# Another set of whole tiles, other slots for some jobs, and one ScalarE raise for two heads

## The reference, cut to what matters

```python
ffn  = lambda z: z @ W.T + b + (z @ V_r) @ C.T                # rank 32
x = x + 0.5 * ffn(ln(x))                                      # stage A
q, k, v = split(ln(x) @ W_attn)                               # stage B, 16 heads of 16
s = (q @ k.T) / 4, causal
p = (s*s + 1 if s > 0 else 1 - s/100) / 1000                  # 'polymax', no row sum; for s >= -100
x = x + (p @ v) @ W_proj                                      # stage C
x = x + 0.5 * ffn(ln(x))
```

## Time and profile before

| what | us |
| --- | --- |
| median of 3 runs | 1784.87 (1782.54 to 1789.83) |
| the profiled execution | 1781.97 |
| its span, first to last instruction | 1780.2 |
| TensorE's granted clock, mean over the span | 0.983 |

### The profile page before, as it was taken

How to read it: one execution, slowest core, us unless ns; L and a number is a source line. 1 busy time by engine, 2 the same in 40 slices (tenths; PEclk the granted TensorE clock), 3 DMA queues, 4 the chain that set the end, 5 groups by cost and what they waited for, 6 DMA issues and landing times.

```text
span 1780.2 us, 67010 instructions
## 1 busy us (share of the span) xinstructions
PE 1610.6 (90%) x27158; PEld 834.3 (47%) x27158; DVE 1328.6 (75%) x3272; ACT 1364.4 (77%) x2178; POOL 1319.1 (74%) x1415
## 2 busy tenths in 40 slices
PE   5788889998999999999999999999999989998884
PEld 3444444454545454554545455554545443434342
DVE  4776787778787878787787878778787778786661
ACT  2355668898888888888787887888897879797660
POOL 3456568888988878788897878788796768685652
PEclk9999999999999999999999999999999999999997
DMA  3453343324334252443334152433425141413102
GB/s 95 159 169 120 109 144 89 116 73 123 92 115 127 60 166 72 133 112 110 111 107 138 55 170 77 124 94 110 130 80 147 46 118 41 118 41 94 40 29 64
DMA packets 156857, 183.17 MB, mean 103 GB/s; under 512 B 22140, under 2 KB 129788, under 8 KB 155012
## 3 DMA queue, kind: packets, MB, share of 16 engines
q1 hardware_dynamic: 156548, 178.82, 34.4%
HBM read 101.38 MB, written 76.30 MB: 100 GB/s over the span
## 4 chain that ended last, share of the span: by engine, by line
PE 55%; DVE 16%; ACT 12%; issue 6%; POOL 6%; DMA 3%; SPq 1%; ACTq 0%; POOLq 0%; DVEq 0%
PE y_ps L1079 20%; PE bank L1079 16%; PE score L1079 16%; DVE rp L1012 9%; ACT rp L910 5%; ACT rp L926 3%; POOL rp L807 3%; PE bank L1105 3%; DVE lin L1018 2%; DMA x1c<-x_scratch 2%; POOL z L769 1%; DVE bnst_ln L1037 1%; ACT rp L930 1%; ACT lin L916 1%; POOL rp L782 1%
## 5 line engine op out<-in xcount | busy, mean ns | idle before, releaser
L1012 DVE TENSOR_SCALAR rp<-score 128x512 f32<-128x512 f32 (+2 forms) x1728 | 944.3, 574 | 287.0 <-PE score L1079 284.2
L807 POOL TENSOR_TENSOR rp<-rp 128x1024 f32<-128x1024 f32 (+1 forms) x416 | 757.3, 1829 | 57.9 <-DVE rp L1012 46.1
L1079 PE MATMUL score<-qs,ks 96*32 96x512 bf16 (+3 forms) x10240 | 725.1, 350 | 54.2 <-DVE lin L1018 22.7
L1079 PE MATMUL y_ps<-rp,vt 128*16 128x512 f32 (+3 forms) x5120 | 598.7, 533 | 27.2 <-POOL rp L807 11.3
L910 ACT ACTIVATE rp<-score 128x512 f32<-128x512 f32 (+1 forms) x832 | 463.5, 602 | 201.5 <-PE score L1079 199.5
L1079 PEld LDWEIGHTS score<-qs,ks 96*32 96x32 bf16 x10240 | 303.4, 96 | 432.7 <-DVE rp L1012 146.0
L926 ACT ACTIVATE rp<-rp,rise 128x1024 f32<-128x1024 f32 (+1 forms) x416 | 466.4, 1155 | 0.4 <-POOL rp L782 0.4
L782 POOL TENSOR_SCALAR_AFFINE_SELECT rp<-rp 128x256 f32<-128x256 f32 (+1 forms) x384 | 186.4, 487 | 291.3 <-DVE rp L1012 163.4
L930 ACT ACTIVATE rp<-rp 128x1024 f32<-128x1024 f32 (+2 forms) x224 | 291.8, 1308 | 83.9 <-POOL rp L782 57.2
L1018 DVE SCALAR_TENSOR_TENSOR lin<-score,slope_mask 128x128 f32<-128x128 f32 x768 | 215.3, 280 | 0.0
L1079 PEld LDWEIGHTS y_ps<-rp,vt 128*16 128x16 f32 x5120 | 143.2, 96 | 116.4 <-issue 38.3
(11 more groups left out here) (79 smaller groups left out, 1292.1 us busy)
## 6 DMA issues: line engine op xcount, KB each, us to landing
qs<-part_scratch SPq DMA_DIRECT2D x384, 64.0 KB, 2.4
ks<-part_scratch SPq DMA_DIRECT2D x384, 64.0 KB, 2.4
part_scratch<-parts SPq DMA_DIRECT2D x12, 1536.0 KB, 5.6
state_scratch<-st_new SPq DMA_DIRECT2D x16, 528.0 KB
st<-state_scratch SPq DMA_DIRECT2D x64, 132.0 KB
x_sb<-in_L_attn_x_dram SPq DMA_DIRECT2D x16, 512.0 KB, 4.5
x_scratch<-x SPq DMA_DIRECT2D x16, 512.0 KB, 5.6
qT_scratch<-qkT SPq DMA_DIRECT2D x16, 512.0 KB, 5.6
```

What stands on the lines that cost most here:

```text
L807: pool.tensor_tensor(half, half, half, ALU.mult).then_inc(squared["pool"], 1)
L1012: nc.vector.tensor_scalar(rp[T % RP_BUFS][:, 2 * u + v, off:CH], score[H % S_BUFS][:, v, off:CH], 0.0, RISE, ALU.max, ALU.add).then_inc(ra ...
L1079: return nc.tensor.matmul(*args, start=start, stop=stop, skip_group_check=True)
```

## The change

The list of whole tiles becomes 13 tiles instead of 14, seven off the diagonal (6, 10, 26, 28, 33, 34, 38) and six on it (3, 17, 20, 23, 31, 35). Before, the list was 10, 16, 22, 28, 33, 38 and 2, 3, 9, 11, 20, 23, 35, 39. Seven table entries move by one to three slots. `JOINT` holds the odd halves of the 17 tiles that are off the diagonal and shared; for these `heads_at_once` gives one pair, and so one raise of 1024 columns that waits for the second head's score, and its counters rise by two. `HALVED` is empty; with that, `pool_squares` is the same as `shared`, and the branches for it never run.

```diff
-WHOLE = OFF_DIAG[3::4] + [t for t in DIAG if TILES[t][2] >= 2 * P]
+WHOLE = [3, 6, 10, 17, 20, 23, 26, 28, 31, 33, 34, 35, 38]
+
+HALVED = []
+
+JOINT = [2 * t + 1 for t in OFF_DIAG if t not in WHOLE]
 
 def shared(T):
-    return T % NT not in WHOLE
+    return T % NT not in WHOLE and T % NT not in HALVED
...
+def pool_squares(T):
+    return T % NT not in WHOLE
+
+def heads_at_once(H):
+    return ((0, 2),) if H % NHALF in JOINT else ((0, 1), (1, 2))
...
-A_FULL = {"z1T": (32, 33), "ffn": (36, 40), "z2T": (61, 63), "ln1": 10, "ln2": 45}
-B_FULL = {"qT": (0, 7), "k": (8, 12), "v": (16, 20), "kT": (45, 57), "state": (49, 59, 61, 63)}
-C_FULL = {"proj": (22, 26), "ln3": 30, "z3T": (69, 69), "out": (72, 76)}
+A_FULL = {"z1T": (32, 33), "ffn": (36, 40), "z2T": (63, 63), "ln1": 10, "ln2": 48}
+B_FULL = {"qT": (0, 5), "k": (8, 12), "v": (15, 19), "kT": (43, 55), "state": (49, 59, 61, 63)}
+C_FULL = {"proj": (22, 26), "ln3": 33, "z3T": (69, 69), "out": (72, 76)}
...
-                    for v in range(2):
-                        act.wait_ge(qk_done, 2 * H + v + 1)
-                        nc.scalar.activation(rp[T % RP_BUFS][:, 2 + v, off:CH], score[H % S_BUFS][:, v, off:CH],
-                                             ACT.Relu).then_inc(raised["act"], 1)
+                    for first, last in heads_at_once(H):
+                        act.wait_ge(qk_done, 2 * H + last)
+                        nc.scalar.activation(rp[T % RP_BUFS][:, 2 + first:2 + last, off:CH], score[H % S_BUFS][:, first:last, off:CH],
+                                             ACT.Relu).then_inc(raised["act"], last - first)
```

More of the change, by code:

```diff
@@ L271, in order @@
         squared["act"] += 1
-        squared["pool"] += shared(T)
+        squared["pool"] += pool_squares(T)
         if is_diag(T):
@@ L803, in slot @@
                         mask(buf[:, :, off:off + P], QH)
-                    if shared(T):
+                        if pool_squares(T):
+                            pool.wait_ge(masked, o.masked[T] + 1)
+                    if pool_squares(T):
                         wait_raised(pool, H - 1)
@@ L915, in slot @@
                                 act.wait_ge(pv_done, diag_tile(D - L_BUFS) + 1)
-                            nc.scalar.activation(lin[D % L_BUFS][:, 2 + v, :], score[H % S_BUFS][:, v, off:off + P],
-                                                 ACT.Copy, scale=SLOPE, bias=ONE).then_inc(lin_done["act"], 1)
+                            nc.scalar.activation(lin[D % L_BUFS][:, 2 + first:2 + last, :], score[H % S_BUFS][:, first:last, off:off + P],
+                                                 ACT.Copy, scale=SLOPE, bias=ONE).then_inc(lin_done["act"], last - first)
                 for T in o.squares.get(s, ()):
@@ L921, in slot @@
                         act.wait_ge(masked, o.masked[T] + 1)
-                    if shared(T):
+                    if pool_squares(T):
                         wait_raised(act, 2 * T + 1)
                         part = rp[T % RP_BUFS][:, 2:4, off:CH]
-                        nc.scalar.activation(part, part, ACT.Square, bias=rise[:]).then_inc(squared["act"], 1)
+                        if shared(T):
+                            nc.scalar.activation(part, part, ACT.Square, bias=rise[:]).then_inc(squared["act"], 1)
+                        else:
+                            nc.scalar.activation(part, part, ACT.Square).then_inc(squared["act"], 1)
                     else:
@@ L1009, in slot @@
                         dve.wait_ge(pv_done, T - RP_BUFS + 1)
[L1010 to L1013, removed]
+                    for first, last in heads_at_once(H):
+                        heads = slice(2 * u + first, 2 * u + last)
+                        dve.wait_ge(qk_done, 2 * H + last)
+                        nc.vector.tensor_scalar(rp[T % RP_BUFS][:, heads, off:CH], score[H % S_BUFS][:, first:last, off:CH],
+                                                0.0, RISE, ALU.max, ALU.add).then_inc(raised["dve"], last - first)
                         if is_diag(T):
@@ L1017, in slot @@
                                 dve.wait_ge(pv_done, diag_tile(D - L_BUFS) + 1)
-                            nc.vector.scalar_tensor_tensor(lin[D % L_BUFS][:, 2 * u + v, :], score[H % S_BUFS][:, v, off:off + P],
-                                                           ONE / SLOPE, slope_mask[:, 0, :], ALU.add, ALU.mult).then_inc(lin_done["dve"], 1)
+                            nc.vector.scalar_tensor_tensor(lin[D % L_BUFS][:, heads, :], score[H % S_BUFS][:, first:last, off:off + P],
+                                                           ONE / SLOPE, slope_mask[:, first:last, :], ALU.add, ALU.mult).then_inc(lin_done["dve"], last - first)
                 for x in o.empties.get(s - 1, ()):
```

## The result

| | us |
| --- | --- |
| before, median of 4 | 1787.35 |
| after, median of 4 | 1771.95 |
| ratio | 0.9922, 95% interval 0.9895 to 0.9950 |
| the two profiled executions | 1781.97 and 1772.74 |

The forecast was 1759, a change of -1.5% from the median that stood there then; measured is -0.8%.

A forecast was written before the change was run, and what follows sets the result against it. TensorE was taken as the bound, losing about 9 us of each 101 us full iteration, mostly waiting for VectorE. Terms by place and iteration summed to -22.8 us on 1781.97, giving 1759 (own range 1743 to 1774).

The forecast's parts named there:

- full iterations, 4 to 10: Seven iterations with all tables: -2.0 us each from the places and the joint raise, -14 together.
- without C: Three iterations lacking the last stage's table: -1.2 us each, -3.6 together, as tiles 33 to 35 have less cover.
- 12 to 14: Late iterations with only the C table: -1.0 us each, from the start, tiles 15 to 24, ScalarE and joint raise.
- Halves 60 to 72: Late in a full iteration, around z2T and tiles 33 to 35: +0.5 us, bounds -0.8 and +3.
- wait for z: At half 63, z2T's transposes wait 1.0 us for GpSimd's last normalisation, the second transpose in that wait's shadow.
- Halves 40 to 59: Tiles 20 to 29 of a full iteration: loss from 4.2 to 3.2 us, -1.0, bounds -3 and +1.5.
- Halves 0 to 6: Start of an iteration: VectorE comes 0.8 us earlier, loss 1.5 to 0.3, -1.2, bounds -1.5 and +0.3.
- Halves 30 to 39: Tile 16 shared, tile 17 whole: loss from 1.0 to 0.6 us, -0.4, bounds -0.8 and +0.6.
- The joint raise: ScalarE raises two heads at once on 17 shared off-diagonal tiles: +0.1 us per iteration, bounds -0.9 and +2.8.
- The second rival: Slower by the joint raise, which holds scores in half of 272 pairs: 45 us come, 1803; chance 0.06.
- The third rival: Slower by z2T: GpSimd's backlog makes both transposes wait 5.8 us in ten iterations, 1807; chance 0.10.
- The first: Rival: the loss only moves, VectorE's two buffers being the real limit, about 1778 to 1784 us; chance 0.20.

The follow-up runs named there:

- list alone: Kernel before with only the new list of whole tiles (old slots, heads one by one): 1.0023 of the kernel before.
- slots alone: Kernel before with only the three new slot tables (old list, heads one by one): 1.0036 of the kernel before.

## Why the prediction had the direction and not the size

Its terms against the two profiles, in us:

| step | forecast | measured |
| --- | --- | --- |
| full iterations, 4 to 10 | -14 | -7.7 (709.8 to 702.1), of which 2.4 by one iteration that was longer before |
| without C, 1 to 3 | -3.6 | -2.4 |
| number 11 | -1.2 | -0.4 |
| 12 to 14 | -3 | +2.1 |
| 15 | -1 | -5.1 |
| iteration 0 and start; tail | 0 | +3.9; +0.4 |
| sum | -22.8 | -9.2 |

The full iteration carries the largest part of the miss: -2.0 was forecast, and it went from 101.0 to 100.3 or so. The part on the places says why, and the -9.2 has luck in it: -5.1 in number 15, where -1 was forecast for another reason, is more than half of it.

**Halves 60 to 72 (the term that was mis-sized most).** Forecast +0.5, of which the wait for z 1.0; measured +1.5 to +1.8 in 60 to 69. The wait for z was foreseen to the instruction: z was to be ready 21 us after tile 23's start, and was after 21.06 (1016.27 less 995.21), and the wait was 0.97. But the second transpose, which I had put in its shadow, waited another 0.51, through VectorE's `st_add`, for the state's addition on GpSimd. And half 63 was reached after 19.3 instead of 20, and I took wait and stretch for separate prices. The runs show one thing in their place: GpSimd has no slack from half 46 to 62 (0.17 us), and ln3 at 33, which I had put among four contributors at 40 to 59, is worth 1.6 us of each full iteration. The recorded sum for GpSimd there doesn't come out of its own terms: three squares, four biases, four normalisations and two split steps make 12.7, not 15.8. The shared tiles among 21 to 25 are four (21, 22, 24, 25); the fourth square and tile 23's mask make it 15.2, and the trace has GpSimd busy from 992.88 to 1008.06, 15.2 us, with no break over 0.1. So the size of the backlog was about right, and its price was not.

**Halves 40 to 59.** Forecast -1.0, measured -1.2 to -1.7. The size held, and so did the late squares of 24 and 25: TensorE's values start 0.14 after each ended. That tile 22 and the statistics are the reason fits the list alone, which has ln2's statistics beside tile 23 and loses 3.8 in 50 to 59, but no run moved them alone. Halves 10 to 29 and 70 to 79, at nothing in the sum, gave 0.3 and 0.1.

**Halves 0 to 6.** Forecast -1.2, because VectorE would come 0.8 earlier; measured -0.6, and by the slots alone, with the old list. I had read VectorE's lateness of 1.5 at half 0 as the cause of the gap at half 4. But the two qT pieces of halves 0 and 1 cover it, and at half 2 the raise started 0.2 after its score: the gap is the chain from that score through two raises and two lines (1.33 us) to the next, with no job beside it. In the changed kernel it stands there still: half 4 loses 0.56, as before. What was gained is half 6, filled by qT's piece.

**Halves 30 to 39.** Forecast -0.4, measured +0.1: the same total of VectorE's work, one tile later. With ln3 at 30 the list gives -0.25 (0.80). (The 3.06 us that the prediction has for tile 16 hold two statistics, not three; the third stands in the next tile.)

**The joint raise.** Forecast +0.1 per iteration, measured 0.2 to 0.7. The second rival had the mechanism and, at 45 us, ten times the price: the runs give 4 and 10 us, half of the 10 outside iterations 1 to 14. My ground against it, that no matmul row names that raise, was a row of the kernel before, where the raise frees the first head early.

**The late iterations, and the last.** The new list brings nothing in 12 to 14 (list and slots without the joint raise: 98.3, 88.0, 89.9 against 97.3, 88.4, 89.1). It brings 5 us in the last one of the two first profiles, where I had looked at engines' loads only and not at the loads of x1c; about 1 us of it is left at the same time at the lower clock, and that the shorter waits are what spares the rest is not shown. Iteration 0, at nothing in the sum, costs about 3 us by the list, as the table above has it, while executions of the same instructions differ by 3 to 7.

Of the signs that were named, the full iteration came at 100.0 to 100.4, neither 99 nor above 100.5; the gap in halves 2 to 6 stayed; values that wait for GpSimd's square became fewer, not more (14 times, 18 before); and the sign against the joint raise came, scores that wait for it.

The third rival (z2T decides, slower) has its mechanism in the traces, with a wait of 1.0 where it asked 5.8. The first, that the loss only moves, holds within halves 46 to 69, on GpSimd and not, as I had it, on VectorE.

## What to carry to other kernels

When a job's table entry moves, add up what it issues on the least watched engine in the window it lands in, against TensorE's time for that window: here ln3, moved by three slots, cost 1.6 us of each full iteration, 1.3 of it put down to GpSimd, where the whole change gained 0.7. A wait that the profile names for an engine late in a stretch may be the last sign of a backlog; to find its price take away the work, not the wait, and read from a window how much idle time that engine has left. Where the row names another engine, look at what that one waited for: here two waits under two names, z and `st_add`, both ended in GpSimd's queue. And a lateness that precedes a gap isn't its cause if the engine has caught up in between: read the delay at the last instruction ahead of the gap.

## What the runs showed that was not expected

The same instructions in iterations 1 to 10 repeat to 0.1 us in most executions, while iteration 0 and the last one, where the granted clock falls to half in stretches of 3.4 to 6.8 us after TensorE has idled, differ by 3 to 7 us. Such a stretch can stand elsewhere too: three profiles have 3.4 us of it in iteration 14, which then lasts 92.6 to 92.7 us, against 88.2 to 90.9 in the others. With kernels as near as these, a difference of a median within that isn't a difference of the schedule; the length of one full iteration tells them apart at 0.1 us, and the ends can be compared at the same time at the lower clock.
